# Norms in halves, with the next stage's loads, weight splits and router inside them, and products of zeros among the narrow ones

## The chip, the cores and the metric

One Trainium2 chip, one of its NeuronCores. The metric is the time of one execution on the device in microseconds (us), as the median of several runs. TensorE (PE) multiplies, VectorE (DVE), ScalarE (ACT) and GpSimd (POOL) do the element-wise work, SyncE (SP) issues transfers.

## The reference, cut to what matters

Four layers of attention and feed-forward on a residual x of 1024 tokens by 256 features, in float32:

```python
x = x + _L0_attn_ref(_layernorm(x, axis=-1), ...)
x = x + _L0_ffn_ref(_layernorm(x, axis=-1), ...)    # routed experts, 16 of them, and a shared one
x = x + _L1_attn_ref(_layernorm(x, axis=-1), ...)
x = x + _L1_ffn_ref(_layernorm(x, axis=-1), ...)    # attention, an RMS norm of its own, a gated MLP
x = x + _L2_attn_ref(_layernorm(x, axis=-1), ...)
x = x + _L2_ffn_ref(_layernorm(x, axis=-1), ...)    # routed experts, 32
x = x + _L3_attn_ref(_layernorm(x, axis=-1), ...)   # a layernorm inside it as well
x = x + _L3_ffn_ref(_layernorm(x, axis=-1), ...)    # routed experts, 16, chosen by groups
```

A layernorm subtracts the mean over the 256 features of a token and multiplies by the inverse root of the variance. In a routed layer a small product (the router) gives each token's logits, the largest experts are chosen and their weights scale the expert outputs.

## The kernel before, in words

x lies on the chip transposed: features on the 128 partitions, in DC = 2 blocks, and T = 1024 tokens along the row, in NH = 2 halves of 512 and TB = 8 blocks of 128. Products that need float32 precision are made of three passes: weights and activations are split into a high part (fp32r) and a low part, and `gemm3` adds high x high, low x high and high x low.

The program is a chain of stages, and each stage is one or more blocks. A block holds one instruction list for each engine, in the order written, and ends when all its engines are through; the next block begins after that. So nothing of a stage, not even its first weight load, is issued before the norm ahead of it is over.

`norm` runs ten times: n0a, n0f, n1a, n1f, n1r, n2a, n2f, n3a, l3a_ln, n3f (n1r does not subtract a mean; l3a_ln also applies a gain and a shift). In one norm TensorE makes the means of both halves as wide products with a matrix of 1/256 (L128), ScalarE squares each half in one instruction (L199), TensorE sums the squares token block by token block with one moving column each (L137: 16 products, written as 32 instructions, since a float32 product is two), ScalarE takes the root (L202, which needs another activation table than the stage before had), VectorE inverts it (L160), TensorE spreads the inverse over the partitions by a product with the identity (L145), VectorE scales (L166), and the result x_norm is split into x_norm_h (ACT, L208) and x_norm_l (half on POOL, L191, half on DVE, L176; with a gain all on DVE, L182). All sums of squares of both halves stand in TensorE's list ahead of the first spread.

The stages that follow a norm begin like this. `project` (layer 0, layer 1 twice) loads four weight chunks, rope tables and value weights, splits the first chunks and fills ones beside the values. `decay_attention` (layer 3) loads four weight parts and splits them. `moe` (f0, f1, f2, f3) loads two weight chunks and the router's weights, runs the router on TensorE (L380), and its POOL splits chunk 0 (L63, L357, L359) before TensorE's first expert product (L391). In f2 the expert weights are wanted right after chunk 0, and so TensorE waits for VectorE's chain from the logits (L528 to L587). `low_rank` stands ahead of f1. `layer1_mlp` has a block of its own that loads gains (L2970) ahead of n1f, and one that adds r to x (L2979) after n1r. `out_product` already has four products with the zero matrix at its head (L2015).

Of the kernel before, what the change touches and what calls it, by code (L numbers as in the profile page):

```python
# [33 lines left out]
def half(h):  # L34
    return slice(h * HALF, (h + 1) * HALF)
# [68 lines left out]
def norm(nc, core, name, src, center, eps, dst=None, gain=None, split=True, shift=None):  # L104

# [4 lines left out]
    with ExitStack() as ctx:  # L110
# [4 lines left out]
            sem, ("rstd", "spread", "xn", "hi", "lo", "scaled"))  # L115
        sq = sb("sq", [P, DC, T])
        std = sb("std", [P, TB])
        rstd = sb("rstdv", [P, TB])
        xc = sb("xc_b", [P, DC, T]) if center else src
        block = ctx.enter_context(nc.Block())  # L120
        HB = TB // NH

        @block.tensor
        def _(pe):
            if center:
# [6 lines left out]
            for h in range(NH):  # L132
                pe.wait_ge(sq_ready, h + 1)
                for b in range(HB):
                    t = h * HB + b
                    for c in range(DC):
                        mm = pe.matmul(core.bank[2 + h][:, b:b + 1], sq[:, c, t * P:(t + 1) * P],  # L137
                                       core.mean_w[:, 0:1], start=c == 0, stop=c == DC - 1)
                mm.then_inc(var_ready, 1)

            for h in range(NH):
                pe.wait_ge(rstd_ready, h + 1)
                for b in range(HB):
                    t = h * HB + b
                    mm = pe.matmul(core.bank[4 + h][:, b * P:(b + 1) * P], rstd[:, t:t + 1].to_broadcast([P, P]),  # L145
                                   core.ident[:, :], start=True, stop=True)
                mm.then_inc(spread, 1)

        @block.vector
        def _(dve):  # L150
            if center:
# [5 lines left out]
            for h in range(NH):  # L157
                dve.wait_ge(std_ready, h + 1)
                bl = slice(h * HB, (h + 1) * HB)
                dve.reciprocal(rstd[:, bl], std[:, bl]).then_inc(rstd_ready, 1)  # L160
            for h in range(NH):
                dve.wait_ge(spread, h + 1)
                if center:
                    dve.wait_ge(xc_ready, DC * (h + 1))
                for c in range(DC):
                    dve.tensor_tensor(dst[:, c, half(h)], xc[:, c, half(h)], core.bank[4 + h][:, :],  # L166
                                      ALU.mult).then_inc(xn_ready, 1)
                if shift is not None:
                    dve.wait_ge(xn_ready, DC * (h + 1))
                    for c in range(DC):  # L170
                        dve.tensor_scalar(dst[:, c, half(h)], dst[:, c, half(h)], gain[:, c:c + 1],
                                          shift[:, c:c + 1], ALU.mult, ALU.add).then_inc(scaled, 1)
# [14 lines left out]
        def _(pool):  # L187
            if split and gain is None:
# [6 lines left out]
        def _(act):  # L195
            for h in range(NH):
                if center:
                    act.wait_ge(xc_ready, DC * (h + 1))
                act.activation(sq[:, :, half(h)], xc[:, :, half(h)], ACT.Square).then_inc(sq_ready, 1)  # L199
            for h in range(NH):  # L200
                act.wait_ge(var_ready, h + 1)
# [55 lines left out]
def moe(nc, core, name, w_dram, n_chunks, n_ahead, kind=None, E=16, top_k=0, gate_w=None, bias_row=None, sel_w=None,  # L257
        b2_dram=None, shared=0, z_h=None, z_l=None):
# [12 lines left out]
    with ExitStack() as ctx:  # L271
# [19 lines left out]
        if routed:  # L291
# [25 lines left out]
            if b2_dram is not None:  # L317
# [3 lines left out]
                cwr = sb("cwr", [P, T], F32R)  # L321
        block = ctx.enter_context(nc.Block())
# [14 lines left out]
        @block.sync  # L337
        def _(sp):
            def load(c, i, slot):
                if not isinstance(c, int) or c >= 2:  # L340
                    sp.wait_ge(raw_free, c - 1)
                sp.dma_start(raw[:, slot, :], w_dram[c]).then_inc(w_in[slot], 16)
            chunks(sp, load)

        @block.gpsimd
        def _(pool):
            if routed:
                pool.memset(parts[:, :, :], 0.0).then_inc(made, 1)
                pool.wait_ge(made, 1)
                pool.memset(parts[:, :, 96:97], 1.0).then_inc(made, 1)  # L350

            def split(c, i, slot):
                pool.wait_ge(w_in[slot], i * 16 + 16)
                if not isinstance(c, int) or c >= 2:
                    pool.wait_ge(y_done, c * 2 - 2)
                core.pool_copy(pool, wh[:, slot, :], raw[:, slot, 0:B]).then_inc(w_split, 1)
                pool.tensor_copy(bias[:, slot, :], raw[:, slot, B:B + 2]).then_inc(w_split, 1)  # L357
                pool.wait_ge(w_split, c * 3 + 2)
                pool.tensor_tensor(wl[:, slot, :], raw[:, slot, 0:B], wh[:, slot, :].bitcast(F32),  # L359
                                   ALU.subtract).then_inc(w_split, 1)  # L360
                pool.wait_ge(w_split, c * 3 + 3)
                pool.sem_inc(raw_free, 1)
# [2926 lines left out]
```

## Time and profile before

| | |
|---|---|
| median of 3 runs | 2912.28 us (2910.21 to 2912.98) |
| profiled execution, own time | 2908.62 us |
| its span | 2906.9 us |
| PE busy / DVE / ACT / POOL | 88% / 56% / 44% / 44% of the span |
| granted TensorE clock, mean over the span | 0.914 |

The profiled execution's time is its span and 1.7 us around it, and it lies 3.7 us below the median. Durations are read from this one execution. The granted clock is given as a share of full speed: 1.00 is 2.4 GHz, 0.50 is 1.2 GHz. A busy TensorE is not one at its peak: a matmul of one column counts as busy as one of 512. Where TensorE stands still, the granted clock of a stretch costs nothing.

### The profile page before, as it was taken

The numbers are of one execution on the slowest core, as the hardware profiler recorded it, in microseconds if no ns is written. First come the engines' busy times: TensorE is split into PE (matmuls) and PEld (weight loads), VectorE is DVE, ScalarE is ACT, GpSimd is POOL, SyncE is SP. The second block draws the span as 40 slices with busy tenths as digits, with TensorE's granted clock in tenths as the row PEclk, the third lists the DMA queues.
The fourth block names the chain that finished last, engine by engine and source line by source line (L and its number), as shares of the span: only waits on it lengthen the run. The fifth ranks groups of instructions, "written<-read, shape, count | busy, mean of one in ns | idle before, by whom it ended". The sixth has DMA issues, their size and how long they took to land. (4 is left out here: it accounts for less than half of the span.)

```text
span 2906.9 us, 41109 instructions
## 1 busy us (share of the span) xinstructions
PE 2564.2 (88%) x14578; PEld 1712.5 (59%) x14578; DVE 1621.6 (56%) x2144; ACT 1264.1 (43%) x2133; POOL 1273.2 (44%) x1110
## 2 busy tenths in 40 slices
PE   6887899785999999999868877889999988997798
PEld 4443677552444444444554435678888866775576
DVE  4653355465666766664335533477777745554455
ACT  4454333362555555545324652245655542332232
POOL 3000344273888888888411002255544523441143
PEclk8788899896999999999976978989999998998699
DMA  1000111113011011010000001010000001110011
GB/s 49 1 1 8 42 49 43 44 42 79 23 30 37 23 37 37 15 30 1 29 16 1 1 6 42 23 47 26 19 30 19 23 1 40 49 43 15 23 44 42
DMA packets 40143, 82.18 MB, mean 28 GB/s; under 512 B 7856, under 2 KB 21424, under 8 KB 39472
## 3 DMA queue, kind: packets, MB, share of 16 engines
q1 hardware_dynamic: 37392, 76.25, 9.3%
q10 hardware_dynamic: 2592, 3.82, 0.4%
q8 instruction: 99, 1.62, 0.2%
q14 instruction: 60, 0.49, 0.1%
HBM read 60.12 MB, written 3.15 MB: 22 GB/s over the span
## 5 line engine op out<-in xcount | busy, mean ns | idle before, releaser
L1866 DVE TENSOR_REDUCE a1h_mseg<-bank 128x2 f32<-128x1024 f32 x256 | 302.3, 1222 | 185.2 <-PE bank L1631 177.0
L1793 ACT ACTIVATE a1h_prob<-bank 128x512 f32<-128x512 f32 x440 | 246.6, 598 | 191.8 <-PE bank L1687 105.4
L1615 POOL TENSOR_TENSOR a_qk<-a_qk,a1h_prob 128x512 f32<-128x512 f32 x230 | 298.3, 1329 | 49.1 <-ACT a1h_prob L1793 49.1
L63 POOL TENSOR_TENSOR f_wh<-f_raw,ones_r 128x768 fp32r<-128x768 f32 (+1 forms) x74 | 111.3, 1504 | 409.2 <-PE bank L402 372.8
L391 PE MATMUL bank<-x_norm_h,f_wh 128*128 128x512 f32 x592 | 242.1, 409 | 10.0 <-POOL f_wl L359 9.8
L391 PE MATMUL bank<-x_norm_l,f_wh 128*128 128x512 f32 x592 | 237.2, 401 | 0.0
L391 PE MATMUL bank<-x_norm_h,f_wl 128*128 128x512 f32 x592 | 236.4, 399 | 0.0
L600 DVE SCALAR_TENSOR_TENSOR f_tf<-bank,f_bias,f_sg 128x512 f32<-128x512 f32 x148 | 111.0, 751 | 203.2 <-PE bank L391 182.4
L1700 PE MATMUL bank<-a1h_prob,a_v 128*64 128x512 f32 x880 | 215.0, 603 | 0.0
L1685 PE MATMUL bank<-a1h_ql,a1h_k 128*128 128x512 f32 x512 | 202.1, 395 | 0.0
L488 ACT ACTIVATE f_hhi<-f_hf 128x512 fp32r<-128x512 f32 x124 | 78.3, 632 | 271.7 <-DVE f_hf L608 271.5
L614 DVE TENSOR_TENSOR f_hlo<-f_hf,f_hhi 128x512 fp32r<-128x512 f32 x124 | 112.0, 904 | 82.8 <-ACT f_hhi L488 82.5
L477 ACT ACTIVATE f_sg<-bank,f_bias 128x512 f32<-128x512 f32 x148 | 101.7, 687 | 129.6 <-PE bank L391 129.6
L1615 POOL TENSOR_TENSOR x_norm<-x_norm,a1h_prob 128x512 f32<-128x512 f32 x104 | 134.8, 1332 | 24.7 <-ACT a1h_prob L1793 24.5
L391 PEld LDWEIGHTS bank<-x_norm_h,f_wh 128*128 128x128 f32 x592 | 113.5, 192 | 51.9 <-issue 13.2
L402 PE MATMUL bank<-f_hhi,f_wh 128*128 128x512 f32 x296 | 118.6, 401 | 13.8 <-DVE f_hlo L614 13.8
L359 POOL TENSOR_TENSOR f_wl<-f_raw,f_wh 128x768 fp32r<-128x768 f32 (+1 forms) x74 | 127.7, 1725 | 5.9
L391 PEld LDWEIGHTS bank<-x_norm_l,f_wh 128*128 128x128 f32 x592 | 113.5, 192 | 28.0
L391 PEld LDWEIGHTS bank<-x_norm_h,f_wl 128*128 128x128 f32 x592 | 113.9, 192 | 25.2
L1684 PE MATMUL bank<-x_norm_h,a1h_kn 128*128 128x512 f32 x256 | 119.4, 467 | 5.1 <-DVE a1h_k L1854 3.4
L2646 POOL TENSOR_TENSOR l2a_rope<-l2a_rope,l2a_tab 128x512 f32<-128x512 f32 x64 | 81.3, 1279 | 90.0 <-ACT l2a_rope L2523 89.1
L1363 ACT ACTIVATE a2h_prob<-bank 128x512 f32<-128x512 f32 (+3 forms) x192 | 83.7, 488 | 82.0 <-PE bank L1174 57.4
(568 smaller groups left out, 6230.4 us busy)
## 6 DMA issues: line engine op xcount, KB each, us to landing
f_raw<-in_l_w_dram SPq DMA_DIRECT2D x66, 385.0 KB, 3.1
a1h_st_q<-a_qk SPq DMA_DIRECT2D x128, 128.0 KB, 2.4
a_qk<-l_keys SPq DMA_DIRECT2D x32, 128.0 KB, 2.6
l2a_qkraw<-in_l2a_wqk_dram SPq DMA_DIRECT2D x32, 128.0 KB, 2.1
l2a_vraw<-in_l2a_wvg_dram SPq DMA_DIRECT2D x8, 512.0 KB, 3.7
f_raw<-in_l_w_dram SPq DMA_DIRECT2D x8, 449.0 KB, 3.3
a1p_raw<-in_l1a_w_dram SPq DMA_DIRECT2D x20, 128.0 KB, 2.1
l_keys<-a_qk SPq DMA_DIRECT2D x4, 512.0 KB, 4.0
```

The source lines that it names most:

```text
L63: return pool.tensor_tensor(dst, src, one.to_broadcast(list(src.shape)), ALU.mult)
L359: pool.tensor_tensor(wl[:, slot, :], raw[:, slot, 0:B], wh[:, slot, :].bitcast(F32), ALU.subtract).then_inc(w_split, 1)
L391: mm = pe.matmul(out[:, :], w[:, slot, c0:c0 + P], x, start=n == 0, stop=n == 3 * n_k - 1)
L402: mm = pe.matmul(acc[m][h][:, :], w[:, slot, c0:c0 + P], x[:, h, :], start=begin and n == 0, stop=False, skip_group_check=True)
L600: dve.scalar_tensor_tensor(tf[:, h, :], up[h][:, :], bias[:, slot, 1:2], sg[:, h, :], ALU.add, ALU.mult).then_inc(t_ready, 1)
L614: dve.tensor_tensor(hl[:, h, :], src[:, h, :], hh[:, h, :].bitcast(F32), ALU.subtract).then_inc(hl_ready, 1)
L1615: pool.tensor_tensor(out, first, slot_of[t % NP], ALU.add).then_inc(sum_done, 1)
L1684: pe.matmul(bank[:, :], kn[:, G % 2, a, keys], QA[n % 2][:, a, half(h)], start=True, stop=False)
L1685: mm = pe.matmul(bank[:, :], k1[:, a, keys], ql[:, n % 2, a, half(h)], start=False, stop=lo >= hi)
L1700: pe.matmul(core.bank[5][64 * a:64 * a + 64, :], v[:, kb, 2 * (n // 4) + a, :], slot_of[t % NP], start=kb == 0, stop=kb == TB - 1, skip_gr ...
L1793: act.activation(slot_of[t % NP], core.bank[2 + t % 3][:, :], ACT.Exp, scale=scale).then_inc(p_ready, 1)
L1866: dve.tensor_reduce(mseg[:, :, qb, s], spare(("A", n, k))[:, :, :], AX.X, ALU.max).then_inc(a_read, 1)
```

## The change

1. `norm` works by halves further down its chain. The squares are four instructions in place of two; TensorE's list is: means, 3 dense products, sums of blocks 0 and 1, 2 dense, sums of blocks 2 and 3, 2 dense, sums of blocks 4 and 5, spread of half 0, sums of blocks 6 and 7, 3 dense, spread of half 1. A dense product is zero matrix x 512 columns of x_norm_h, written to bank 6, which nobody reads; n0a has none. VectorE scales half 0 before it inverts half 1. A root of one column at the start of ScalarE's list brings the table early. The spread is a transposing matmul.
2. The stage after a norm is handed to it as functions (`sync`, `gpsimd`, `tensor`): the norm's block issues the next stage's loads on SP (those that ACT issued too), splits the first weights on POOL (moe: chunk 0; project: 2 chunks with rope, 4 without, and the fill of ones; decay attention: 2 of 4 parts), and runs the router at the end of TensorE's list. `low_rank` does the same for f1. The attention of layer 2 (n2a) gets nothing.
3. `layer1_mlp` loses its two small blocks: the gains are loaded inside n1f, and r is added to x by VectorE inside `project`.

```diff
@@ norm @@
+    def dense(count):
+        for _ in range(count if warm else 0):
+            pe.matmul(core.bank[6][:, :], core.zero_r[:, :], core.xh[:, 0, half(1)], start=True, stop=True)
...
+    def spread_inverse(h):
+        pe.wait_ge(rstd_ready, h + 1)
+        for b in range(HB):
+            t = h * HB + b
+            mm = pe.transpose(core.bank[4 + h][:, b * P:(b + 1) * P], rstd[:, t:t + 1].to_broadcast([P, P]),
+                              core.ident[:, :])
+        mm.then_inc(spread, 1)
...
+    dense(3)                       # centered norms only
+pe.wait_ge(sq_ready, DC)
+for t in range(HB):
+    mm = sum_squares(t)
+    if t % 2:
+        mm.then_inc(var_ready, 1)
+        dense(2)
+pe.wait_ge(sq_ready, 2 * DC)
+sum_squares(HB)
+sum_squares(HB + 1)
+spread_inverse(0)
+sum_squares(HB + 2)
+sum_squares(HB + 3).then_inc(var_ready, 1)
+dense(3)
+spread_inverse(1)
+if tensor is not None:
+    tensor(pe, xn_ready)
...
+invert(0)
+scale(0)
+invert(1)
...
+scale(1)
...
+act.activation(root[:, :], eps[:, :], ACT.Sqrt).then_inc(root_loaded, 1)
+for n in range(DC * NH):
+    h, c = n // DC, n % DC
+    act.activation(sq[:, c, half(h)], xc[:, c, half(h)], ACT.Square).then_inc(sq_ready, 1)
@@ moe @@
+def first_loads(sp):
+    load(sp, 0, 0)
+    if routed:
+        sp.dma_start(gw[:, :, :], gate_w).then_inc(gate_in, 16)
+    load(sp, 1, 1)
...
+def first_split(pool):
+    if routed:
+        pool.memset(parts[:, :, :], 0.0).then_inc(made, 1)
...
+    split_weights(pool, 0, 0, 0)
+def router(pe, normed):
+    pe.wait_ge(gate_in, 16)
+    for t in range(TB):
+        if t % (TB // NH) == 0:
+            pe.wait_ge(normed, DC * (t // (TB // NH) + 1))
...
-                if routed and isinstance(c, int) and c == 0:
+                if routed and isinstance(c, int) and c == 1:
                     pool.wait_ge(sel_in, 16)
@@ project @@
+def first_splits(pool):
+    for c in range(AHEAD):
+        pool.wait_ge(w_in[c], 16)
+        core.pool_copy(pool, wh[:, c, :], raw[:, c, 0:WC]).then_inc(w_hi, 1)
...
+    if fill is not None:
+        pool.memset(fill, 1.0).then_inc(filled, 1)
...
+            if added is not None:
+                x, r = added
+                dve.tensor_tensor(x, x, r, ALU.add).then_inc(sum_made, 1)
```

## Rows read from the trace of the kernel before

**Rows 1.** Windows, each norm's last work to the next stage's first product: length, busy, PEclk.
```profile
24.42:32.16 7.74, 0.00 (x1) 0.00 (x1) 0.70 (x2) 3.46 (x5) 0.72 (x1) 0.50 0.70 255
300.99:313.14 12.15, 6.85 (x33) 6.85 (x33) 0.00 (x1) 1.28 (x1) 7.68 (x11) 0.50 0.40 117
558.16:566.21 8.05, 0.00 (x0) 0.01 (x1) 1.23 (x1) 1.92 (x4) 0.72 (x1) 0.52 0.73 262
1494.15:1502.43 8.28, 0.00 (x1) 0.00 (x1) 3.10 (x3) 2.54 (x2) 1.57 (x2) 0.50 0.31 95
1775.96:1783.53 7.57, 0.00 (x0) 0.00 (x0) 0.01 (x1) 0.00 (x0) 3.88 (x3) 0.57 0.37 121
2408.66:2419.55 10.89, 7.07 (x33) 7.07 (x34) 0.00 (x1) 1.28 (x1) 7.85 (x9) 0.50 0.42 119
2658.05:2663.37 5.32, 0.00 (x1) 0.00 (x1) 0.01 (x1) 0.99 (x2) 1.26 (x1) 0.50 0.63 182
2729.25:2739.59 10.34, 6.86 (x33) 6.86 (x33) 0.28 (x2) 1.28 (x1) 7.74 (x9) 0.50 0.40 124
```

**Rows 2.** Timeline of norm n1a: start us, us, engine, line, operation, idle before.
```profile
545.16 1.28 DVE L155 TENSOR_TENSOR n1a_xc_b<-x_resid,bank 128x512 f32<-128x512 f32 x2 [4.58 <-PE bank L128]
...
547.58 3.73 PE L137 MATMUL bank<-mean_w,n1a_sq 128*128 128x1 f32 x32 [0.75 <-ACT n1a_sq L199]
...
549.27 1.28 ACT L202 ACT_TABLE_LOAD   x1
...
551.18 3.38 PE L145 MATMUL bank<-ident,n1a_rstdv 128*128 128x128 f32 x16
...
552.89 1.28 DVE L166 TENSOR_TENSOR x_norm<-n1a_xc_b,bank 128x512 f32<-128x512 f32 x2 [1.06 <-PE bank L145]
...
555.80 2.36 DVE L176 TENSOR_TENSOR x_norm_l<-x_norm,x_norm_h 128x512 fp32r<-128x512 f32 x2
```

**Rows 3.** Windows of six norms, from first centering (n1r: first square) to last work.
```profile
11.72:24.42 12.70, 8.59 (x52) 6.63 (x51) 7.66 (x12) 6.37 (x9) 2.85 (x2) 0.79 0.00 0
1465.45:1478.37 12.92, 11.08 (x52) 9.20 (x51) 5.49 (x10) 3.92 (x5) 0.00 (x0) 0.70 0.00 0
1478.67:1494.15 15.48, 10.40 (x48) 10.11 (x48) 5.57 (x10) 5.19 (x8) 0.00 (x0) 0.65 0.01 1
2393.81:2408.66 14.85, 10.51 (x52) 8.92 (x50) 7.67 (x12) 6.38 (x9) 2.85 (x2) 0.76 0.00 1
2642.34:2658.05 15.71, 11.46 (x52) 9.46 (x51) 7.67 (x12) 6.38 (x9) 2.86 (x2) 0.72 0.00 0
2686.52:2699.91 13.39, 9.75 (x52) 8.16 (x50) 7.41 (x14) 3.92 (x5) 0.00 (x0) 0.70 0.00 0
```

**Rows 4.** Windows inside norms n2f and n1r: sums of squares at the two clocks.
```profile
2396.24:2398.50 2.26, 2.26 (x19) 2.26 (x20) 0.57 (x1) 1.64 (x2) 0.00 (x0) 0.94 0.00 0
1479.78:1486.56 6.78, 6.78 (x33) 6.78 (x33) 0.18 (x1) 1.15 (x2) 0.00 (x0) 0.52 0.00 0
```

**Rows 5.** Windows from the last residual add to the first mean product: n1a, then n1f.
```profile
540.58:541.57 0.99, 0.00 (x0) 0.03 (x1) 0.00 (x0) 0.00 (x0) 0.00 (x0) 0.90 0.00 0
1458.54:1461.66 3.12, 0.00 (x1) 0.04 (x1) 0.00 (x0) 0.00 (x0) 0.00 (x0) 0.66 0.02 1
```

**Rows 6.** Timelines elsewhere: transposes, zero products, a head's first split on POOL.
```profile
1732.89 0.63 PE L1277 MATMUL bank<-ident,a2h_ou 128*128 128x128 f32 x4 [0.81 <-ACT a2h_ou L1375]
...
1736.71 2.05 PE L2015 MATMUL bank<-x_norm_h,zero_r 128*128 128x512 f32 x4 [1.26 <-PEq L1084]
...
306.12 1.47 POOL L63 TENSOR_TENSOR f_wh<-f_raw,ones_r 128x768 fp32r<-128x768 f32 x1 [3.73 <-DMA f_raw<-in_l_w_dram]
```

**Rows 7.** The chain that ended last, one of many pieces: twelve wide products at 2.4 GHz.
```profile
2776.26 2.81 PE bank L391 x12
```

**Rows 8.** Window after the head of a1p: its first products.
```profile
566.20:572.00 5.80, 5.79 (x14) 4.59 (x15) 0.70 (x1) 1.55 (x4) 2.74 (x3) 0.50 0.22 71
```

**Rows 9.** Line L600: count, durations min/median/max in ns, first and last start.
```profile
L600 DVE SCALAR_TENSOR_TENSOR f_tf<-bank,f_bias,f_sg x148: 744/751/752, 318.2 to 2894.3; 128x512 f32<-128x512 f32 x148
```

More of the change, by code:

```diff
@@ L121, in norm, with _, sum_squares @@
         HB = TB // NH
+        if sync is not None:
+            @block.sync
+            def _(sp):
+                sync(sp)
         @block.tensor
         def _(pe):
+            def dense(count):
+                for _ in range(count if warm else 0):
+                    pe.matmul(core.bank[6][:, :], core.zero_r[:, :], core.xh[:, 0, half(1)], start=True, stop=True)
+            def sum_squares(t):
+                for c in range(DC):
+                    mm = pe.matmul(core.bank[2 + t // HB][:, t % HB:t % HB + 1], sq[:, c, t * P:(t + 1) * P],
+                                   core.mean_w[:, 0:1], start=c == 0, stop=c == DC - 1)
+                return mm
+            def spread_inverse(h):
[5 more added lines that the diff above has]
+                mm.then_inc(spread, 1)
             if center:
@@ L130, in _, with invert, scale @@
                     mm.then_inc(mean_ready, 1)
[L132 to L147, printed above, removed]
+                dense(3)
[15 more added lines that the diff above has]
+                tensor(pe, xn_ready)
         @block.vector
         def _(dve):
+            def invert(h):
+                dve.wait_ge(std_ready, h + 1)
+                bl = slice(h * HB, (h + 1) * HB)
+                dve.reciprocal(rstd[:, bl], std[:, bl]).then_inc(rstd_ready, 1)
+            def scale(h):
+                dve.wait_ge(spread, h + 1)
+                if center:
+                    dve.wait_ge(xc_ready, DC * (h + 1))
+                for c in range(DC):
+                    dve.tensor_tensor(dst[:, c, half(h)], xc[:, c, half(h)], core.bank[4 + h][:, :],
+                                      ALU.mult).then_inc(xn_ready, 1)
             if center:
@@ L375, in _ @@
         def _(pe):
-            if routed:
-                pe.wait_ge(gate_in, 16)
-                for t in range(TB):
-                    for c in range(DC):
-                        mm = pe.matmul(logits[:, t, :], core.xn[:, c, t * P:(t + 1) * P], gw[:, c, :],
-                                       start=c == 0, stop=c == DC - 1)
-                mm.then_inc(logits_ready, 1)
             def gemm(out, cols, n_k, slot, h):
@@ L723, in _ @@
             def _(pool):
-                load_split((None, None, pool), raw, wh, wl, srcs, w_in, hi, lo, None)
+                for j in range(AHEAD, 4):
+                    low(pool, j)
             @block.tensor
@@ L885, in _ @@
         def _(sp):
-            def load(c, i, slot):
-                sp.wait_ge(raw_free, c + 1)
-                sp.dma_start(raw[:, slot, :], w_dram[c]).then_inc(w_in[slot], 16)
-            chunks(sp, load)
+            if ROUNDS > 1:
+                with sp.Fori(0, ROUNDS - 1) as i:
+                    for slot in range(SLOTS):
+                        c = i * SLOTS + (SLOTS + slot)
+                        sp.wait_ge(raw_free, i * SLOTS + (slot + 1))
+                        sp.dma_start(raw[:, slot, :], w_dram[c]).then_inc(w_in[slot], 16)
         @block.gpsimd
         def _(pool):
-            pool.sem_inc(raw_free, SLOTS)
             pool.sem_inc(sin_done, 2)
@@ L912, in _ @@
                 with_splits_ahead(pool, lambda c, i, slot: split_low(pool, c, i, slot), times_sin)
-            else:
-                chunks(pool, split)
         @block.tensor
@@ L985, in _ @@
                 chunks(act, evacuate)
-            for memory, value in fills[1:]:
-                act.activation(memory, value, ACT.Copy).then_inc(filled, 1)
         @block.vector
```

244 lines of the change are left out of this document (127 added, 117 removed).

## The prediction

> **What bounds the kernel now.** I read the page first: TensorE is busy 88% of the span and no other engine 60%. That is an average over stages, so I asked for the stretches that the diff touches, which are the ten norms and the head of each stage behind one. A window over each gap between a norm's last work and the next stage's first product [rows 1] shows what such a head is: in five of eight TensorE does nothing, in f0, f2 and f3 it runs the router for 6.9 to 7.1 us at 1.2 GHz, and the rest is a load landing and POOL splitting it. All of this stands on the path, since a block begins only when the one before is over. The eight heads are 70.3 us long together. The timeline of n1a [rows 2] then shows the norm: TensorE's sums (3.73 us) run past ScalarE's table load, the spread follows the last sum, VectorE scales behind it and makes the low parts at the end. It is one chain over four engines, 545.16 to 558.16. Windows over the norms [rows 3] show the same chain at 12.7 to 15.7 us. Windows inside them [rows 4] say where the difference comes from: at 2.4 GHz the narrow sums cost 2.26/19 = 0.12 us each, at 1.2 GHz 6.78/32 = 0.21. In n2f the clock fell while TensorE was working without a gap at narrow products, soon after its last wide one.
>
> **Heads (the loads, splits and router moved into the norm).** What is left of a head is a block's end and a start, for which I take 0.4 us. The heads sum to 70.3, so 70.3 - 8 x 0.4 = 67.1 us goes. It is free only if the moved work fits beneath the norm.
> - POOL: the zeroing of parts, a wait for the load, and three instructions. In the head of f0, POOL starts the split 5.1 us after the norm's last work [rows 1, 6], and is busy 7.7 us over the whole head, for two chunks and the small casts [rows 1]; one chunk is 1.47 + 0.2 + 1.8 us. So about 8.6 us after the norm's start POOL is free, and its own first work, x_norm_l, comes some 12 us after it (3.6 for the means [rows 2, 5], then 8.5). What queues behind the new wait for the load is x_norm_l, and the block's end waits for that. In a2p POOL splits four chunks and fills the ones: 3.5 + 4 x 1.5 + 2 = 11.5 us under a norm that has no low part on POOL; it fits, barely.
> - SP: up to eight issues of half a microsecond at the norm's start, where SP had nothing. The transfers run while no other does. ACT loses its issues.
> - VectorE beside POOL: an operation that reads PSUM kept 744 to 752 ns in all 148 cases, many under POOL's splits [rows 9], and centering and scaling are of that kind. I cost them nothing.
> - The router: TensorE runs 32 narrow products at the end of its norm list, half 0 right after the last spread and half 1 after x_norm's last scaling. At 0.116 us each it ends about when the low parts do; at 0.215 it ends 3.4 us later. With the clock falling halfway, 1.0 us in each of three: -3.
> - f2 needs the logits, and not the product: VectorE's chain starts at the block's start. The table load for its exponential (1.28 us in the head, hidden so far) now shows by 0.4. In f3 and f0 the product of chunk 0 covers it. The later split of chunk 1 on POOL (3.2 us) is wanted by TensorE more than 5 us later.
> - The two small blocks: 3.12 us stand ahead of n1f's mean products where n1a has 0.99 [rows 5], so the gains' block costs 2.1. The add of r is in the head of a2p (counted) and moves under a2p's products, where VectorE's next work waits for the value products behind all four chunks.
> Heads: 67.1 + 2.1 - 0.4 - 3 = 65.8.
>
> **Norms.** From the first centering (0), at 2.4 GHz: the second mean pair ends at 1.7, three dense products (0.235 each by twelve in 2.81 [rows 7]) at 2.4; sums of two blocks are eight instructions, 0.93; two dense 0.47. So sums 2.4 to 3.3, dense 3.8, sums 4.7, dense 5.2, sums 6.1, spread of half 0. Four transposes took 0.63 [rows 6], where the product form needed 1.2 from its start until VectorE went on: 6.8. Scaling to 8.1, inverse, sums until 7.5, dense 8.2, spread of half 1 at 9.1, scaling 10.4, low parts 2.2 with POOL beside them (2.36 in [rows 2]): 12.6. The root's early table load takes 1.28 us out of ScalarE's queue, but the sums take its place; that is why a norm that kept its clock (13.0 in n1a, 12.7 in n0f and n2a) gains only 0.1 to 0.4. What gains is a norm that lost it [rows 3]: n2f 2.2, n3a 2.2 (the slow means delay the new list by 0.9), n3f 2.1, l3a_ln 1.7, n1f 2.0, n1r 3.2 (bounded by POOL). n0a, without dense products, gains 1.3. Sum 15.3, if the clock holds. If it falls as before, spreads, sums and the dense products behind 6 us run at half speed, 2.0 us more: n0f, n1a and n2a lose 1.6 to 1.9 each, n1r 1.3, the others about nothing, and the sum is -5.
>
> Dense products: the diff puts a wide one at most 2 us behind the last in every norm. The trace has no such mixture. Four zero products took 2.05 us at 1.2 GHz [rows 6], so their price is known (0.43 or 0.235) and their effect is not. I take the holding value, since in n2f 2.3 us of sums without a wide product passed at nearly full clock before it fell [rows 4], and keep the other end.
>
> The Trainium skill, page "TensorE: Matmul & The Clock Gate", section "Why this matters for your kernels", names idle gaps between matmul bursts as what costs the clock. The fall inside n2f's gapless sums [rows 4] differs. By that advice alone the dense products would buy nothing and cost up to 9 norms x 10 x 0.235 = 21 us, and the whole sum would be about 60.
>
> The next stage's first products ran at 1.2 GHz for up to 5.8 us [rows 8], which costs half of that. TensorE now stands still about 4 us before a stage, not 8 to 12, or does the router at half the length. Bounds: nothing (the routed stages had climbed part of the way in the router's time, which can cost them 4 in all) to 8 x 2.2 = 18 gained. I take 4.
>
> **Sum.** 65.8 + 15.3 + 4 = 85 us. The profiled execution would go from 2908.6 to 2823.6 (span 2821.9). It lies 3.7 below the median, so the median goes from 2912.3 to 2827.
>
> **Rivals.**
> A. The narrow stretch stays slow. For it: the mixture is still mostly narrow, and the spread, whose products kept TensorE wide before, becomes half as many instructions. Against it: ten wide products. Then norms -5, router 3 x 3.4 rather than 3, next stages -4: 67.1 + 2.1 - 0.4 - 10.2 - 5 - 4 = 50, 2863. The Trainium skill, same page, Part 4 "PE-mode transpose", says that transposing does not count as PE-busy for the clock; no row here tests it, and by it rival A gets likelier.
> B. The clock lasts from the norm through the router into the next stage: 67.1 + 2.1 - 0.4 - 0.6 + 15.3 + 18 = 101, 2811. For it: the last dense products and transposes now stand about 4 us before the stage, and nothing else comes between in the unrouted ones. Against it: the router is narrow, as the sums are.
> C. The heads go but the time is given back, since the stage waits next for something that did not move: POOL's chunk 1, ScalarE's split of the value weights (now at the block's start), in layer 3 the decay column behind two splits and two table loads. Half of 67 comes back: about 2861. Against it: each of these is ready within 3.5 us of the block's start, and TensorE's first chunk lasts 12 to 24 products, 2.8 to 5.6 us at 2.4 GHz.
> D. Slower than before. One mechanism: the load that POOL waits for lands late, with x_norm_l queued behind it. POOL has about 3.5 us to spare; each us beyond is lost in six norms. To eat 85 us the load must land some 18 us after issue, not 5. That the change does nothing would need the blocks to overlap already, which the idle heads exclude.
>
> **How the numbers follow.** The forecast (clock held in most norms) 0.55, A 0.18, B 0.12, C 0.12, D 0.01, no effect 0.02. The likeliest case gives 2827, and its own range is 2815 to 2842 (heads exact to 5, norms 5 to 15, next stages 0 to 10). The range that holds 8 in 10 reaches from B's 2811, a little above the best, to A's and C's: 2809 to 2861. A measurement of this kernel can tell 0.2%, about 6 us. Faster by more 0.97, within 0.02, slower 0.01.
>
> **What would show it.** After the change: in the heads TensorE's first expert or projection product within 0.5 us of the block's start; L380's products in the norm, 3.7 to 5 us long; POOL's first split ended before x_norm_h; the norms from first centering at 11.3 (n0a) to 13.5 us, PEclk 1.00 from the means to the last spread. Wrong if POOL's wait for a load ends after ScalarE's first high part, if PEclk falls to 0.50 between the dense products (then A), or if TensorE's idle time has moved behind the first chunk (then C).

## The result and the profile after

| | before | after |
|---|---|---|
| median | 2911.24 us, 4 runs (2904.88 to 2912.98) | 2839.85 us, 4 runs (2834.93 to 2842.91) |
| profiled execution, own time | 2908.62 us | 2839.98 us |
| its span, mean granted clock | 2906.9 us, 0.914 | 2838.3 us, 0.927 |

The ratio is 0.9757, with a 95% interval of 0.9737 to 0.9778: faster. The forecast was 2827 (own range 2815 to 2842). Against the 85 us forecast, the medians of this table are 71.4 us apart and the profiled executions 68.6.

The first lines are those of [rows 1] again: windows from a norm's last work to the next stage's first product, in the changed kernel.

```profile
23.02:24.16 1.14, 0.00 (x1) 0.03 (x1) 0.18 (x2) 0.84 (x2) 0.00 (x0) 0.50 0.00 0
294.25:297.61 3.36, 3.04 (x15) 2.96 (x15) 0.00 (x0) 0.04 (x1) 0.01 (x1) 0.50 0.00 0
542.96:544.43 1.47, 0.00 (x1) 0.00 (x1) 0.09 (x1) 1.18 (x2) 0.00 (x0) 0.50 0.00 0
1469.24:1469.95 0.71, 0.00 (x0) 0.03 (x1) 0.00 (x1) 0.34 (x1) 0.00 (x0) 0.50 0.00 0
1740.91:1741.24 0.33, 0.00 (x1) 0.03 (x1) 0.01 (x1) 0.00 (x0) 0.02 (x1) 1.00 0.00 0
2367.36:2368.32 0.96, 0.64 (x4) 0.53 (x4) 0.01 (x1) 0.04 (x1) 0.02 (x1) 0.50 0.00 0
2605.19:2605.52 0.33, 0.00 (x1) 0.03 (x1) 0.01 (x1) 0.02 (x1) 0.00 (x0) 0.50 0.00 0
2665.94:2669.30 3.36, 3.04 (x15) 2.96 (x15) 0.00 (x0) 0.04 (x1) 0.01 (x1) 0.50 0.00 0
```

They add up to 11.66 us, where the eight of [rows 1] had 70.3: 58.7 us are gone. A head in which nothing is late is 0.33 us long. Three are longer because TensorE still works in them (f0, f3: 3.04 us of router at PEclk 0.50; f2: 0.64), two because ScalarE does (a0p and a1p, below), and a2p because TensorE's first product waits for a signal that ScalarE gives at the start of the block (0.71). The DMA share is 0.00 in all: no head waits for a transfer any more.

Next the windows over norms, the first six those of [rows 3] in their order (l3a_ln is told below), then n0f and n3f.

```profile
11.50:23.02 11.52, 6.92 (x44) 5.13 (x43) 7.59 (x12) 5.25 (x10) 5.95 (x5) 0.78 0.30 113
1440.70:1452.20 11.50, 9.87 (x54) 7.52 (x53) 5.41 (x10) 3.00 (x7) 0.00 (x0) 0.80 0.00 0
1452.30:1469.24 16.94, 11.79 (x47) 10.60 (x47) 5.58 (x10) 5.25 (x11) 7.09 (x9) 0.50 0.17 47
2354.30:2367.36 13.06, 13.06 (x85) 10.89 (x84) 7.58 (x12) 5.25 (x10) 6.29 (x5) 0.89 0.09 33
2591.80:2605.19 13.39, 9.80 (x54) 7.78 (x52) 7.64 (x12) 5.24 (x10) 7.48 (x6) 0.75 0.22 64
...
280.83:294.25 13.42, 13.42 (x73) 11.77 (x72) 7.68 (x12) 5.25 (x10) 5.81 (x5) 0.75 0.07 22
2652.80:2665.94 13.14, 13.14 (x74) 11.48 (x72) 7.59 (x12) 5.25 (x10) 6.28 (x5) 0.77 0.17 46
```

Against the lengths of before, n0a gains 1.2 us, n2f 1.8, n3a 2.3, n3f 1.6, n1f 1.7 (its last scaling ends 11.2 us after its first centering, before the window's end) and l3a_ln 2.4 (11.0 from first centering to last shift). n0f, n1a and n2a lose 0.7, 0.5 and 0.7, and n1r loses 1.5: its window stands at 0.50 from end to end. Together the norms gain 7.7. Why they gain no more is in TensorE's timeline of n0f.

```profile
283.90 0.71 PE L134 MATMUL bank<-x_norm_h,zero_r 128*128 128x512 f32 x2
284.46 0.95 PE L138 MATMUL bank<-mean_w,n0f_sq 128*128 128x1 f32 x8
...
286.61 0.63 PE L146 MATMUL bank<-ident,n0f_rstdv 128*128 128x128 f32 x4
287.08 1.23 PE L138 MATMUL bank<-mean_w,n0f_sq 128*128 128x1 f32 x8
...
288.17 1.63 PE L134 MATMUL bank<-x_norm_h,zero_r 128*128 128x512 f32 x3
...
289.59 1.05 PE L146 MATMUL bank<-ident,n0f_rstdv 128*128 128x128 f32 x4
290.44 6.85 PE L403 MATMUL bank<-f_gw,x_norm 128*128 128x16 f32 x32
```

L134 are the products of zeros, L138 the sums, L146 the spreads, L403 the router. Windows of one microsecond over the same place give the granted clock (PEclk) as the third number from the end:

```profile
286.00:287.00 1.00, 1.00 (x11) 1.00 (x11) 0.00 (x0) 0.00 (x0) 0.00 (x0) 1.00 0.00 0
287.00:288.00 1.00, 1.00 (x11) 1.00 (x9) 0.72 (x2) 0.00 (x0) 0.00 (x0) 0.80 0.00 0
288.00:289.00 1.00, 1.00 (x4) 0.90 (x5) 0.75 (x2) 0.66 (x2) 0.00 (x0) 0.50 0.00 0
```

From the centering on the mixture of sums and products of zeros ran at 2.4 GHz, and then the clock fell all the same, in the last sums. The second spread takes 1.05 us and not 0.63, and the router 6.85. In n0f, n1a, n1f, n2a, n3a and n3f the last spread took 1.05 us at 0.50; only n2f and l3a_ln reached it at 1.00. A second profile of the same kernel has n1f and n3a at 1.00 as well, and so gives the price of the fall: n1f 9.8 us against 11.2, and n3a 12.06 against the 13.39 above, with the same 54 products.

```profile
2601.53:2613.59 12.06, 8.47 (x54) 6.63 (x52) 7.58 (x12) 5.25 (x10) 7.45 (x6) 0.91 0.24 73
```

The head of a1p, in its timeline, shows the one wait that the change uncovered:

```profile
543.25 1.06 ACT L1058 ACTIVATE a1p_vh<-a1p_vraw 128x1024 fp32r<-128x1024 f32 x1 [1.91 <-PEq L110]
...
544.43 0.79 PE L725 MATMUL bank<-x_norm_h,a1p_wh 128*128 128x512 f32 x1 [5.07 <-DVEq L1074]
```

L1074 is VectorE's signal that the banks are free. It stands in VectorE's list behind a wait for the high part of the value weights (L1058), which ScalarE makes at the block's start. TensorE's first product waits for a signal that has nothing to wait for.

### The profile page after: what moved, and what is told of

The parts are those of the page before. It is cut to its first block and busy times, and to the rows that moved or that the text cites. A ratio compares the mean times of both kernels' runs of the same rounds, so it can differ in the third digit from the quotient of the medians.

```text
span 2838.3 us, 41088 instructions
## 1 busy us (share of the span) xinstructions
PE 2552.9 (90%) x14585; PEld 1698.8 (60%) x14585; DVE 1627.4 (57%) x2144; ACT 1261.3 (44%) x2154; POOL 1282.1 (45%) x1118
## 5 line engine op out<-in xcount | busy, mean ns | idle before, releaser
L1764 PE MATMUL bank<-x_norm_l,a1h_kn 128*128 128x512 f32 x256 | 118.6, 463 | 0.9
```

Of the source, the lines that this page charges most:

```text
L1764: pe.matmul(bank[:, :], kn[:, G % 2, a, keys], QA[n % 2][:, a, half(h)], start=True, stop=False)
```

## The experiments

The runs were measured in three groups: first heads only, norms only, no products of zeros and the router at the head; then the tail, more zeros, the product spread and small; then the rest. Each is compared with runs of the kernel before on the same chip in its group, and ratios and intervals refer to these. The median of before was 2909.33 us in the first group, 2907.74 in the second, 2901.91 in the third. Because whole times turned out to move by some 10 us with stages that no edit touches, the verdicts on one place rest on this table, worked out from the timelines: the microseconds from each norm's first centering to the next stage's first product (norm and head together; n1f holds n1r too), their sum, and what is left of the span. The head of f1 and the block of the gains are in that rest: 9.2 us of it in the kernel before went with the change, which leaves 0.8 of the 10.0 us between the first two lines. Each line is one profile, and an unaltered kernel moves too: compare the second and the third.

```
                  n0a   n0f   n1a   n1f   n2a   n2f   n3a l3a_ln  n3f    sum    rest
before           20.5  24.8  21.0  37.0  15.8  25.5  21.1  16.5  25.1  207.3  2699.6
after            12.7  16.8  14.9  29.3  16.7  14.0  13.7  14.1  16.5  148.7  2689.6
after, again     15.0  16.8  14.9  27.9  16.7  14.0  12.4  14.0  16.1  147.8  2699.7
heads only       17.0  16.2  17.3  26.1  16.0  16.3  13.1  16.3  15.2  153.4  2695.2
norms only       21.8  25.5  19.9  36.8  16.6  23.9  17.2  14.1  23.6  199.4  2694.8
no zero products 15.0  14.9  15.4  24.9  14.7  17.3  14.2  13.9  16.6  146.7  2694.2
router at head   12.6  20.6  14.9  27.9  16.9  20.7  13.9  16.4  19.2  163.0  2688.7
tail of zeros    12.8  16.3  15.1  29.3  16.8  15.6  13.9  14.8  14.5  149.0  2690.0
more zeros       13.4  15.9  15.8  31.3  16.7  17.0  14.6  15.3  15.8  155.8  2680.9
product spread   14.1  13.9  15.6  29.9  16.4  14.3  13.4  15.0  13.5  145.9  2689.3
small            14.6  16.8  14.0  25.5  16.9  16.9  13.8  14.0  16.5  149.0  2701.1
twice            13.9  13.7  15.6  29.6  16.5  14.1  13.3  14.8  13.2  144.8  2680.3
product, no zero 16.9  19.1  17.2  28.4  16.2  19.2  16.0  15.3  16.3  164.6  2693.2
put together     12.2  14.1  14.2  25.7  15.3  13.4  12.4  14.8  13.4  135.5  2684.6
```

**Heads only.** The functions handed to the norm stay, with the norm's inside as before (no products of zeros, product spread, all sums ahead of the first spread, late table).

```diff
 def norm(..., sync=None, gpsimd=None, tensor=None, warm=True):
-    # body of the changed kernel
+    # body of the kernel before, with sync(sp), gpsimd(pool) and tensor(pe, xn_ready) called in it
```

> All of the change except the norm's inside: loads, first splits and router are inside the norms, the block of the gains is gone, but squares, sums, roots and spreads run in the order of the kernel before, without products of zeros, without the early square-root table and with the old spread. If the heads carry the gain, as the comparison of the two traces says (58.7 us of heads and 2.1 of the gains block), about 2911 - 61 = 2850 us, ratio to before 0.979. If the new order inside the norms is worth the 15.3 us that the prediction gave it, 2855 to 2858. If the two halves of the change need one another (the old norm, longer by its late table and its slow sums, hides the loads better, so that the order inside adds nothing), 2840 to 2843.

2852.88 us (2850.11 to 2855.14), ratio 0.9806 (0.9778 to 0.9835), between the first two forecasts. The table has 53.9 us less than before, without f1's head and the gains' block. Two routers run at full clock here with no product of zeros: behind the old spread of 16 instructions in one piece the router takes 3.87 us in f2 and 4.03 in f3 (6.98 in f0). In n3f:

```profile
2672.29 3.76 PE L151 MATMUL bank<-ident,n3f_rstdv 128*128 128x128 f32 x16
2675.85 4.03 PE L373 MATMUL bank<-f_gw,x_norm 128*128 128x16 f32 x32
```

**Norms only.** The kernel before with the new inside of `norm`, nothing handed to it; n0a has no products of zeros.

> The reverse: the kernel before with only the new inside of the norm (order by halves, table first, transposes, products of zeros), no load, split or router moved, the gains block still there. If parts add up, and the norms gain what the traces show (7.7 us), about 2903 us, ratio 0.997; by the prediction's 15.3 us 2896. A rival: the clock that the products of zeros hold up also reaches the routers at the head of the mixtures (10 us of narrow products at half rate in three stages), then 2890 or less. Another: the heads wait for loads, not for the norm, and nothing moves: 2911.

2897.52 us, ratio 0.9959 (0.9941 to 0.9978): 11.8 us less, of which the table finds 7.9. The two parts measured alone sum to 56.5 + 11.8 = 68.3 us, the whole to 71.4. Within their intervals (8 us for heads, 5 for norms) they add up, so no need of one for the other shows, and heads are about five sixths of it. The time lies nearer to the forecast with 15.3 us (2896) than to the one with 7.7 (2903), the table at 7.9; the rest of the span was 4.8 us shorter than in the profile of before. The router at the head keeps half clock (374 to 422 ns for each of its instructions), so the rival that it profits falls.

**No products of zeros.**

```diff
-            for _ in range(count if warm else 0):
+            for _ in range(0):
```

> The changed kernel with no products of zeros at all (7 to 10 of 128x512 fewer in each centred norm). If they earn their place, sums at half rate cost 1.64 us a block instead of 0.95 (four blocks: 2.8 us) against the 2.1 us of TensorE time that the products of zeros take between them: 0.5 to 1.5 us more in each of nine norms and the router of f2 at half rate (2.4 us): 2847 to 2852. If what they take is as much as what they bring, 2838 to 2843. If they hold back the roots more than they help, below 2836.

2842.63 us, ratio 0.9771 (0.9743 to 0.98), not to be told from the changed kernel. By place n0f, n1f, n2a and n1r are some 2 us shorter without them (n1f only 0.6 against the second profile of the changed kernel), n2f is 3.2 longer (its router falls to half clock), the other norms within 0.5 (n0a never had any). In n0f the clock falls 7 to 8 us after the first centering with them and without.

**Router back at the head** of f0, f2 and f3, loads and splits still in the norm.

```diff
-            before(sync=first_loads, gpsimd=first_split, tensor=router)
+            before(sync=first_loads, gpsimd=first_split)
...
         def _(pe):
+            if routed:
+                router(pe)
```

> The changed kernel with the router's 32 products back at the head of the three routed mixtures; loads and splits stay inside the norms. The norm's block then ends 3.0 us sooner in f0 and f3 and 1.0 in f2, and the router takes 6.85 us (4.4 to 6.9 in f2) before the first product: by this 3.6 + 3.6 + 5 = 12 us more, 2852 us. The rival: the narrow products run faster there or the head waits for something else anyway, 3 us or less more in each: 2845 or less.

2852.54 us, ratio 0.9813 (0.9783 to 0.9844), 12.7 us more than the changed kernel's first median, as forecast. The three places cost 3.8 + 6.7 + 2.7 = 13.2 more. The timeline after n0f:

```profile
294.48 6.98 PE L401 MATMUL bank<-f_gw,x_norm 128*128 128x16 f32 x32 [3.91 <-PEq L110]
301.30 0.77 PE L463 MATMUL bank<-x_norm_h,f_wh 128*128 128x512 f32 x1
```

The narrow products run at half rate there as well. Moving the router is worth 13 us of the 71.

**A tail of zeros, and more of them.** Both add wide products behind the last spread, where TensorE waits for VectorE, and between the router's blocks. The second also has four in place of two behind each pair of sums of half 0 and two behind the first spread.

```diff
             spread_inverse(1)
+            if split:
+                pe.wait_ge(hi_ready, DC)
             if tensor is not None:
+                fill(2)                    # fill: zero matrix x x_norm_h, half 0
-                tensor(pe, xn_ready)
+                tensor(pe, xn_ready, fill) # fill(1) behind each block of half 0, every second of half 1
+            elif split:
+                fill(12)
```

> The changed kernel with more products of zeros, all behind the last spread, where TensorE waits for VectorE: 12 in the unrouted norms, 2 plus 6 among the router's products in the routed ones. In the changed kernel the clock falls at the second spread, the router takes 6.85 us at half rate in f0 and f3, and each stage's first products run at half rate. If wide products there bring the clock back before the router is through, the router gains 1 to 3 us in each of two stages and 2 to 3 us come back behind each of seven heads: 2815 to 2830. If the clock does not return in so short a stretch, the added products cost 0.43 us each in the router's list (6 of them, three times: 5 to 8 us): 2845 to 2848.

> As the run with a tail of products of zeros, and four in place of two after each pair of sums of half 0 and two after the first spread: 6 more wide ones, 1.4 us more of TensorE time in each norm. If more of them hold the clock through the norm, the last three products of zeros take 0.7 instead of 1.6 us, the second spread 0.6 instead of 1.05 and the router about 3.7 instead of 6.85: some 2 to 8 us less than with the tail alone. If the clock falls at the same place whatever stands there, 10 to 14 us more than the tail alone.

The tail: 2831.85 us (2826.31 to 2846.21), ratio 0.9744 (0.9714 to 0.9774); its interval overlaps that of the changed kernel, and the time lies between the two forecasts. At the places the router ends earlier in f3 (2.0 us) and later in f2 (1.6), and the sum is as before. What the tail does show is the clock behind it: the first 5.8 us of a1p held 25 products at PEclk 1.00, where the changed kernel has 14 at 0.50.

More: 2844.47 us, 0.9783 (0.9758 to 0.9808). They hold the clock at the last spread in all eight centered norms that have products of zeros, and in n0f through the router and into f0: a window over the first 5.9 us of f0 held 18 products at PEclk 0.69 in the changed kernel and 24 at 1.00 here.

```profile
297.61:303.50 5.89, 5.89 (x18) 4.71 (x19) 3.49 (x10) 3.53 (x5) 4.78 (x6) 0.69 0.46 133
```
```profile
298.24:304.10 5.86, 5.86 (x24) 4.40 (x24) 4.60 (x24) 4.73 (x6) 4.76 (x6) 1.00 0.44 134
```

But TensorE is in the norm's chain there, and each added product of zeros delays it: norms and heads cost 7 us more in sum. The forecast had 2 to 8 us less than the tail alone if the clock held; it held, and the median is 12.6 more. The rest of the span was the second shortest of the table (2680.9), but by less than such a rest moves in one kernel. So the clock can be held by such products, and at this count no gain shows.

**Product spread.**

```diff
-                    mm = pe.transpose(core.bank[4 + h][:, b * P:(b + 1) * P], rstd[:, t:t + 1].to_broadcast([P, P]),
-                                      core.ident[:, :])
+                    mm = pe.matmul(core.bank[4 + h][:, b * P:(b + 1) * P], rstd[:, t:t + 1].to_broadcast([P, P]),
+                                   core.ident[:, :], start=True, stop=True)
```

> The changed kernel with the spreads as products with the identity again, as in the kernel before. By duration alone each half's spread takes 1.2 instead of 0.63 us at full clock and 1.7 to 2.1 instead of 1.05 at half: about 1.1 us more in each of ten norms, 2851 us. If the products keep the clock up where transposes let it fall (the Trainium skill, page TensorE: Matmul & The Clock Gate, Part 4, says that transposing does not count as busy for the clock), the fall at the second spread goes, the routers of f0 and f3 gain 3 us each and the norms 1 us each: 2836 to 2842.

2844.85 us (2836.95 to 2849.05), ratio 0.9787 (0.9761 to 0.9812): no difference in the whole, and between the two forecasts. By place the clock is plain. TensorE's timeline in n0f:

```profile
293.02 1.14 PE L146 MATMUL bank<-ident,n0f_rstdv 128*128 128x128 f32 x8
294.00 0.95 PE L138 MATMUL bank<-mean_w,n0f_sq 128*128 128x1 f32 x8
294.81 0.93 PE L134 MATMUL bank<-x_norm_h,zero_r 128*128 128x512 f32 x3
295.63 1.16 PE L146 MATMUL bank<-ident,n0f_rstdv 128*128 128x128 f32 x8
296.62 3.64 PE L403 MATMUL bank<-f_gw,x_norm 128*128 128x16 f32 x32
300.70 0.47 PE L462 MATMUL bank<-x_norm_h,f_wh 128*128 128x512 f32 x1 [0.44 <-PEq L110]
```

The router takes 3.64 us and not 6.85, the head 0.3, in all three routed stages: n0f and n3f are 2.9 and 3.0 us shorter, n2f even. All eight centered norms with products of zeros reach their last spread at 1.00. The unrouted ones pay up to 1 us each for the longer spread.

**Transposes twice.** Is it the kind of work, or how much of it there is? The same transposes, each issued twice.

```diff
-                for b in range(HB):
+                for b in [*range(HB), *range(HB)]:
```

> The changed kernel with every transpose of the spreads done twice, into the same place: eight for each half, as many as the instructions of the product form, and about as long (1.26 us at full clock). With the product form the clock stood at 1.00 through the norms and routers of f0, f2 and f3 and the head there was 0.3 us. If that came from the kind of the work, doubled transposes leave the fall where the changed kernel has it, near the second spread, with the router at 6.85 us in f0 and f3: heads 3.4 us, norms 1.5 to 2.5 us longer, 2855 to 2862. If any wide work of that length does it, heads of 0.3 us as with products: 2840 to 2850.

2837.85 us (2826.76 to 2844.14), ratio 0.9784 (0.9767 to 0.9802), against 2840.35 and 0.9784 of the changed kernel in the same group. The time is below both forecasts and decides nothing. In n0f:

```profile
286.50 1.07 PE L146 MATMUL bank<-ident,n0f_rstdv 128*128 128x128 f32 x8
...
288.22 0.95 PE L134 MATMUL bank<-x_norm_h,zero_r 128*128 128x512 f32 x3
289.04 1.09 PE L146 MATMUL bank<-ident,n0f_rstdv 128*128 128x128 f32 x8
289.96 3.64 PE L403 MATMUL bank<-f_gw,x_norm 128*128 128x16 f32 x32
```

The clock holds as with products: at the last spread of all eight centered norms with products of zeros, where two profiles of the changed kernel have it in two and in four. I had put the kind first in the expectation; the rival came. The Trainium skill, page "TensorE: Matmul & The Clock Gate", Part 4 "PE-mode transpose", says that for the clock transposing "doesn't count as PE-busy the same way"; this run speaks against it, since four transposes more in each spread are all that differs from the kernel whose router took 6.85 us. They also move what stands behind them by 0.4 us; no run separates that from the work itself.

**Product spread without products of zeros.** Both edits shown above.

> Spreads as products and no products of zeros at all. If the products of the spread alone hold the clock until the router is through, the products of zeros buy nothing: heads of 0.3 us in f0, f2 and f3, n1r 2.3 us shorter, the other norms 0 to 1 us shorter, and 3 to 8 us less than the run with the product form and products of zeros. If the clock needs both, PEclk falls to 0.50 in the sums or behind them, routers take 6.85 us (heads 3.4) in at least two of the three, norms 0.5 to 2 us longer: 5 to 15 us more than that run.

2861.53 us (2850.87 to 2869.55), ratio 0.9861 (0.9839 to 0.9884), the slowest with moved heads. In n0f:

```profile
290.21 1.87 PE L138 MATMUL bank<-mean_w,n0f_sq 128*128 128x1 f32 x8 [0.25 <-ACT n0f_sq L239]
291.94 2.06 PE L146 MATMUL bank<-ident,n0f_rstdv 128*128 128x128 f32 x8
...
297.93 6.85 PE L403 MATMUL bank<-f_gw,x_norm 128*128 128x16 f32 x32
```

Here the clock falls in the sums already, and the router takes 6.85 us or more in all three routed stages. So the products of zeros are not idle: in the new order and beside a long spread they keep the norms and routers at full clock and are worth 164.6 - 145.9 = 18.7 us by the table, more than the 5 to 15 forecast. Beside the short spread of the changed kernel the clock falls in most norms anyway, and they are worth nothing that could be measured. The 18.7 are not what the new inside gains over the old: heads only, with the long spread, the old order and no products of zeros, has 153.4. Against that the product spread with products of zeros gains 7.5 us, the changed kernel 4.7 or 5.6, and the new order without them loses 11.2.

**Small.** The signal ahead of the wait, and no products of zeros in n1r.

```diff
+            if rope:
+                dve.sem_inc(out_done, 8)
             dve.wait_ge(v_split, 1)
...
-            if rope:
-                dve.sem_inc(out_done, 8)
...
-norm(nc, core, "n1r", r, False, core.eps6, gain=gains[:, 0, :], **ahead)
+norm(nc, core, "n1r", r, False, core.eps6, gain=gains[:, 0, :], warm=False, **ahead)
```

> The changed kernel with two small things undone: in the projections with rope VectorE signals that the banks are free before it waits for ScalarE's high part of the value weights (TensorE's first product waited 0.8 to 1.1 us for that in two stages), and n1r has no products of zeros (its clock stood at 0.50 with them; without, its norm took 14.6 us against 16.9 in the kernel without any). Both by their own places: 2 + 2.3 = 4 us less, 2836 us, and the first products of a0p and a1p within 0.4 us of the block's start. If the wait hides another one (the first weights' low part), nothing moves there.

2845.03 us (2837.5 to 2851.77), ratio 0.9777 (0.9751 to 0.9803): the whole doesn't show it (2836 was forecast). By place both came: the heads of a0p and a1p fell to 0.71 and 0.82 us (1.1 us together), and n1r from 16.9 to 14.6. The rest of its span was 11.5 us longer than in the first profile of the changed kernel, with no edit there.

**The changed kernel again, and one put together**: products in the spreads of the three routed norms, transposes elsewhere, the tail of 12 in the unrouted ones, and both small edits.

```diff
...
+                    if tensor is not None:
+                        mm = pe.matmul(out, inv, core.ident[:, :], start=True, stop=True)
+                    else:
+                        mm = pe.transpose(out, inv, core.ident[:, :])
...
+            if split and tensor is None:
+                pe.wait_ge(hi_ready, DC)
...
+            elif split:
+                fill(12)
```

> The changed kernel once more, unaltered, beside the three others on their chip, so that they can be set against it and not only against the kernel before: 2840 us, ratio 0.976 if the first measurement holds, at most 0.3% off it. Its profile tells how far stages that no edit touched move from one execution to the next: the attention of layer 0 took 257 us from its first product to the next centering in the first profile, and 260 to 266 in four of the others. If that is chance, this profile shows either; if the edits caused it, 257 again.

> A version put together from what the places showed: spreads as products in the three routed norms (n0f 2.9 and n3f 3.0 us less to the first expert product, n2f even), transposes in the others with 12 products of zeros behind the last spread where the high part is made (2 to 6 us less from the first product on in a1p and a2p with f1), no products of zeros inside n1r (2.3), the signal for free banks ahead of the wait in the projections (1.1 together). Sum 11 to 15 us less than the changed kernel: 2825 to 2829 by the runs so far. If only the local gains count that stand in front of a first product (9 us), 2831; if the stages behind give it back by their own clock, no difference from the changed kernel.

The changed kernel: 2840.35 us (2838.18 to 2849.21), 0.9784 (0.9769 to 0.98), within the 0.3% that was forecast. Put together: 2823.48 us (2817.03 to 2832.79), 0.9732 (0.9711 to 0.9753). These two intervals don't touch, and it beats both kernels, the changed one by 16.9 us. Its interval does overlap that of the changed kernel's first measurement (0.9737 to 0.9778) and that of the tail alone (0.9714 to 0.9774). By place it is 12 to 13 us shorter than either profile of the changed kernel: n0f, n3f and n1r as measured singly, together with n1a's head some 8 us; n2a by 1.4 and, against the first profile, n1f and n3a by as much; against the second, n0a by 2.8. No edit stands ahead of the last spread in n2a, n1f, n3a and n0a. The clock held in the first three this time, as it did in n1f and n3a in the second profile of the changed kernel, so this part can be chance. As in the tail run, a1p starts at full clock; windows over the first 5.8 us of a1p, the changed kernel's first:

```profile
544.43:550.20 5.77, 5.77 (x14) 4.51 (x15) 1.84 (x2) 1.54 (x4) 2.74 (x2) 0.50 0.24 72
```
```profile
545.18:551.00 5.82, 5.82 (x25) 4.74 (x26) 3.21 (x4) 4.59 (x9) 4.12 (x4) 1.00 0.24 69
```

## Why the prediction was right, and where not

- **What bounds it: right.** The heads were the gain: 58.7 of 68.6 us by the windows, 56.5 of 71.4 by the run with heads only. The gains' block went for 2.0 us (2.1 forecast): from the last residual add to the mean product n1f now has 1.15 us, where it had 3.12.
- **POOL, SP, the late load (D): right.** In n0f POOL's split lies at 280.36 to 283.87 and the first x_norm_h at 288.50. In n1r the fill of ones ends at 1462.6, ahead of the norm's last work at 1469.2.
- **The router's overshoot: mis-sized.** Forecast were 3 us for three stages, with the clock falling halfway; it is 3.04 + 0.64 + 3.04 = 6.7, since the clock was at 0.50 for the whole router in two (6.85 us; 4.39 in f2).
- **What is left of a head, 0.4 us: right for five, wrong for three.** a0p, a1p and a2p kept 1.14, 1.47 and 0.71, 2.1 us more in sum, for signals behind a wait or at a block's start. The shifted signal gave back 1.1 us in a0p and a1p. I had looked for what moves with the loads, and not for what ScalarE does at the start of the block; before, the load hid it. Together heads came to 58.7 + 2.0 against 65.8.
- **f2's table load: right, with a companion.** The exponential starts 0.38 us behind VectorE's subtraction, where it had followed at once (0.4 forecast). What I missed beside it: VectorE's scaling of the probabilities took 1.02 us where it took 0.43, with POOL's split beside it. TensorE waits for this chain, as before: from f2's first product to the transposes of the expert weights it is 11.2 us, and it was 10.5.
- **Norms, 15.3: the term that was mis-sized most.** It is 7.7. For n0a, n1f, n2f, n3a, n3f and l3a_ln 11.5 was forecast and 11.1 came. n0f, n1a, n2a and n1r were to give the other 3.8 and lost 3.4. "I take the holding value" is the step that failed: the clock fell before or at the second spread in six of the eight centered norms with products of zeros, and in n1r it never rose, so its products of zeros cost 2.3 us and brought nothing. That n1f, n3a and n3f gained about what was forecast although their clock fell is luck, two errors against each other: the held list is faster than I had it (n3a 12.06 us, forecast 13.5), and a fall costs 1.4 us (n1f, n3a), not 2.0. I gave rival A, the slow stretch, all norms or none; it came in most of them, 7 us after the first centering in n0f, later than [rows 4] had it fall. Why beside a short spread: transposes at half the length of the products, which I booked as a gain of 0.6 us each, took the work away that held the clock. The runs with product spreads and with doubled transposes show that: with either, all eight held. Holding it that way hardly shortens the norms themselves, since the longer spread takes the time (n0f 13.55 us with products, 13.41 in the changed kernel); what it gains is the router.
- **Next stages, 4: near nothing.** The spans between, outside norms and heads, lost 0.8 us, less than the 10.1 by which they differ between the two profiles of the changed kernel. The first products of a1p still run at 0.50 (PEclk of the window shown last, as in [rows 8]).
- **Rival C: no.** It wanted half of the heads' 67 us back behind the heads; the spans there are 0.8 us shorter.
- **Rival B** didn't come of the change, but the clock can last that far: the tail run and the version put together start a1p at 1.00.

By terms: 58.7 + 2.0 + 7.7 = 68.4, measured 68.6. For the heads, 65.8 of the 85 us, the mechanism was right. For the clock it was not: the prediction named PEclk at 0.50 between the products of zeros as the sign of rival A, and that is what most norms show. A's price was too high (norms -5 and routers -10.2 forecast, 7.7 and -6.7 measured), so the time came out between the forecast and A's 2863, 2 us inside the end of the range. That it stayed inside owes something to luck.

What stays open is why the clock held to the last spread in n2f and l3a_ln and fell in the six others with the same list, why n1f and n3a differ between two profiles of one kernel, and what sets the 10 us by which untouched stages vary.

## What to carry to other kernels

Where each stage is a block of its own, look at the window between the last work of one and the first product of the next: loads and splits that need nothing of the stage before can be issued inside it, and what remains of a head was 0.33 us here. Then look for signals that stand behind a wait they don't need, since the old head hid them. Shortening TensorE's wide work in a narrow stretch can cost more than it saves, as in n0f and n3f, because the narrow products and the router behind it then ran at half rate; judge such an edit with its neighbours, not by its own duration.

## What the hardware did that I had not expected

- **Stages without an edit move by some us.** The two profiles of the changed kernel differ by 4.2 us in the attention of layer 1 (896.3 and 900.5 us from a1p's first product to n1f's centering, clock 0.96 and 0.95) and by 3.4 from a2p's first product to n2a (360.7 and 364.0). Between kernels the attention of layer 0 moves most: from its first product to the next centering it took 255 to 260 us in nine of the fourteen profiles and 261 to 266 in the others. Below are the changed kernel, the same again, and the one put together: same instructions (1633 products), other clock. The repeat was to tell chance from the edits; it took 257 again, so for this stage that is not settled.

```profile
24.16:280.83 256.67, 210.42 (x1633) 118.44 (x1634) 133.73 (x180) 131.76 (x256) 32.82 (x30) 0.85 0.03 7
```
```profile
26.79:283.60 256.81, 210.62 (x1633) 118.52 (x1634) 133.67 (x181) 131.75 (x256) 32.91 (x30) 0.85 0.03 7
```
```profile
23.82:286.40 262.58, 216.70 (x1633) 120.89 (x1634) 133.90 (x180) 132.30 (x257) 33.16 (x30) 0.81 0.03 7
```

- **n0a has two lengths** from first centering to last low part, 11.52 and 13.85 us in the two profiles of the changed kernel, at a mean granted clock of 0.78 and 0.69. The 1.2 us that n0a seemed to gain are not certain.
- **Doubled transposes keep the clock**, as told above: a spread at full clock takes 1.07 us and not 0.63 in n0f, and the router behind them 3.2 us shorter.
- **An operation of VectorE on SBUF** took 1.02 us in place of 0.43 beside POOL's split in f2 (one case, and the split beside it was not taken away to test it), while centering, which reads PSUM, kept 680 to 689 ns in n1a with POOL at work beside it and without.
